# TensorE takes a slot's piece of the projections ahead of the residual's work and the down projection

## The reference

```python
h = layernorm(x) * (1 + ca) + sa
xn = norm(h) * norm_g + norm_b
# each direction (the second on the reversed sequence):
u, z = split(xn @ Win.T)                      # 256 and 256 channels
u = silu(conv4(u) + convb)
dtr, Bm, Cm = split(u @ Wx.T)                 # 8, 16, 16
dt = softplus(dtr @ Wdt.T + bdt)
h_t = exp(dt_t * A) * h_(t-1) + dt_t * u_t * B_t      # 16 states, 512 steps
y = (sum_n h_t * C_t + u * D) * silu(z);  y = y @ Wout.T
x = x + ga * (h + y_fwd + y_bwd)
h2 = layernorm(x) * (1 + cb) + sb
w = softmax over the two largest of h2 @ gate_w
out = shared(h2) + sum_e w_e * (silu(h2 @ w1_e) * (h2 @ w2_e)) @ w3_e     # hidden size 256
x = x + gb * out
```

## Time and profile before

| | us |
|---|---|
| median of three runs | 2583.36 (2583.35 to 2584.0) |
| the profiled execution, its own time | 2582.57 |
| its span, first to last instruction | 2580.8 |
| VectorE busy | 2284.9 (89%) |
| TensorE busy, matmuls | 2100.5 (81%) |
| GpSimd busy | 1957.8 (76%) |
| ScalarE busy | 1509.0 (58%) |

### The profile page before, as it was taken

The page is one execution under the profiler, slowest core; times in us unless marked ns, Lnnn a source line. Parts: engine busy times, 40 slices in busy tenths (PEclk is TensorE's granted clock), DMA queues, the critical chain, the costliest instruction groups (busy, mean ns, idle before and its releaser), DMA issues. The chain is left out here.

```text
span 2580.8 us, 31577 instructions
## 1 busy us (share of the span) xinstructions
PE 2100.5 (81%) x9893; PEld 1343.5 (52%) x9893; DVE 2284.9 (89%) x3603; ACT 1509.0 (58%) x2468; POOL 1957.8 (76%) x1437
## 2 busy tenths in 40 slices
PE   3677887978788897888879788897878879887868
PEld 1244554545555455555545555454555545555545
DVE  1699998999999899998989899899999989999973
ACT  2546656655566665656666555666556566555633
POOL 1577878778787877878877787877878787787854
PEclk8777998989899898998989899898989989899998
DMA  3334342333433333333333424333332433333310
GB/s 82 128 129 134 105 138 101 116 123 112 136 105 123 118 110 129 114 125 107 116 124 116 140 99 132 107 111 129 115 132 98 138 106 115 128 106 130 112 68 5
DMA packets 120557, 294.32 MB, mean 114 GB/s; under 512 B 18516, under 2 KB 53172, under 8 KB 120388
## 3 DMA queue, kind: packets, MB, share of 16 engines
q1 hardware_dynamic: 120388, 292.30, 33.7%
HBM read 285.91 MB, written 6.34 MB: 113 GB/s over the span
## 5 line engine op out<-in xcount | busy, mean ns | idle before, releaser
L426 POOL TENSOR_TENSOR bt<-v,bb 128x1024 f32<-128x1024 f32 x512 | 1208.4, 2363 | 158.7 <-DVE psA L787 154.6
L787 DVE TENSOR_TENSOR_SCAN psA<-psA,bt 128x512 f32<-128x512 f32 x1024 | 1197.3, 1215 | 100.7 <-POOL bt L426 81.1
L600 ACT ACTIVATE psA<-dt,aneg 128x512 f32<-128x512 f32 x1024 | 688.2, 688 | 813.0 <-DVE g L797 807.4
L987 PEld LDWEIGHTS psY<-ident,g 128*128 128x128 f32 x4096 | 515.4, 151 | 461.8 <-issue 241.6
L987 PE MATMUL psY<-ident,g 128*128 128x128 f32 x4096 | 605.5, 294 | 149.5 <-DVE g L797 149.4
L797 DVE TENSOR_TENSOR g<-psA,cb 128x512 f32<-128x512 f32 x1024 | 672.5, 676 | 0.0
L526 POOL TENSOR_TENSOR act<-pf,gf 128x512 f32<-128x512 f32 x288 | 366.8, 1273 | 248.4 <-DVE pf L882 216.2
L1068 PE MATMUL F<-h2T,w 128*128 128x512 f32 x576 | 333.9, 663 | 90.5 <-DVE pf L882 90.5
L1112 PE MATMUL F<-w,act 128*128 128x128 f32 x2304 | 319.8, 284 | 44.4 <-POOL act L526 41.1
L1112 PEld LDWEIGHTS F<-w,act 128*128 128x128 f32 x2304 | 292.2, 198 | 61.8 <-POOL act L526 55.3
L1071 PE MATMUL F<-h2T,w 128*128 128x512 f32 x576 | 307.5, 616 | 0.0
(11 more groups left out here) (133 smaller groups left out, 1709.1 us busy)
## 6 DMA issues: line engine op xcount, KB each, us to landing
bb<-bc_rows SPq DMA_DIRECT2D x256, 512.0 KB, 3.7
cb<-bc_rows SPq DMA_DIRECT2D x256, 512.0 KB, 3.6
x<-in_L_attn_x SPq DMA_DIRECT2D x16, 256.0 KB, 4.8
xR<-in_L_attn_x SPq DMA_DIRECT2D x16, 256.0 KB, 4.4
out_x<-osb SPq DMA_DIRECT2D x16, 256.0 KB, 4.8
w<-in_L_ffn_ew SPq DMA_DIRECT2D x2, 1024.0 KB
modA<-mod_table SPq DMA_DIRECT2D x16, 128.0 KB, 4.6
bc_rows<-xd SPq DMA_DIRECT2D x32, 64.0 KB, 3.2
```

What stands on the lines that cost most here:

```text
L426: g.tensor_tensor(bt[:, n % 2, :, :], v[d][:, :, :], bb[:, n // 2 % 2, n % 2, :].unsqueeze(1).broadcast_to([P, NH, T]), ALU.mult).then_inc ...
L600: s.activation(psA[:, half * T:half * T + T], dt_[d][:, half, :], ACT.Exp, scale=aneg[d][:, half, n:n + 1]).then_inc(a_s, 1)
L787: w.tensor_tensor_scan(ah, ah, bt[:, n % 2, half, :][:, order], 0.0, ALU.mult, ALU.add)\
L987: last = m.matmul(psY[:, half * T + i * P:half * T + i * P + P], g_[:, n % 2, half, i * P:i * P + P], ident[:, :], is_transpose=True, star ...
```

## The change

On TensorE alone, `ffn_late` moves behind `side` in each slot. `ffn_side` (the backward direction's turn of acc, slots 1 and 2), `sum_y` and `expert_up` stay where they are. No instruction is added or removed, and no wait is changed.

```diff
                     if ffn:
                         ffn_side(b - 1, slot)
-                        ffn_late(b - 1, slot)
                     if scan_:
                         side(b, slot, True, None if last else b + 1, True)
                     if ffn:
+                        ffn_late(b - 1, slot)
                         expert_up(b - 1, slot)
```

## The result

The changed kernel takes 2740.4 us (2739.9 to 2741.0) against 2583.4 us before: 1.061 times as long, 95% interval 1.059 to 1.062, or 157 us more where 112 were forecast. The direction was right, and the time lies 28 us above the range.

The account below looks back on a forecast made before the run. VectorE paces the scan, busy 142 us of a 152.67 us pass. 14 x 6.6 + 0.5 + 15 x 1.3 = 112.4 us on 2582.6 gave 2695, with 0.8 for the median 2696 us; range 2664 to 2712 us.

Parts of the forecast that it names:

- Slot 29: Down block of expert e=7 queues behind Z, which waits for zs; VectorE's sum starts 3.9 us later a pass.
- Slots 17, 20, 23, 25, 27 and 18, by their places: Down blocks end last in their pairs, so sums wait 1.0, 1.0, 0.5, 0.5, 0.2 us; slot 18 gains 0.5.
- Slots 8 to 10: Transposes into h2T wait for xb; ScalarE takes h2T 1.3 us later, arriving whole at the expert's tanh in slot 10.
- The step that failed: Slots 17 and 23: the pair ends where it did, so the sums wait 1.0 and 0.5 us.
- knock-on rival: Last expert's down block in slots 30 and 31 late by 1 us each pass: 2710 us; 6 in 100.
- GpSimd's waits absorb part: GpSimd runs on while VectorE stalls, shrinking VectorE's 4.9 us of waits for bt: 2627 us; 5 in 100.
- Order hardly matters: TensorE takes a ready block past a waiting one, so VectorE's sums wait for nothing: 2583 us; 2 in 100.
- faster: Tanh of z in slot 29 was waiting for TensorE, so earlier Z half 0 saves 1.61 us: 2553 us; 2 in 100.
- Full clock in slot 29: Z and the down block run at full clock, a term of 2.1 for 3.9 us: 2671 us; 6 in 100.
- h2T hidden: The 1.3 us delay of h2T in slots 8 to 10 costs nothing: 2676 us; 7 in 100.
- The wait for the expert sum: Sign: VectorE's wait ahead of the sum grows to about 100 us in the run, longest near 4 us in slot 29.

Follow-up runs that it names:

- the kernel with slot 29 alone: Kernel before, with the piece (`side`) moved ahead of the down projection (`ffn_late`) in slot 29 only; 2638.8 us.
- the fillers: Changed kernel plus idle-time matmuls on TensorE into F1, overwritten later, one in slot 16 and two in slot 21; 2697.5 us.
- The two passes of one execution above: Half-clock and full-clock passes of the kernel before with `side` ahead only in slots 3, 4, 16, 18, 22, 26, 28; 2581.6 us.

## Why the prediction was right and where it was wrong

**Slot 29**: forecast 3.9 us, measured 3.55. The mechanism holds step by step: Z behind zs, the down block behind Z, the wait for tanh unchanged, TensorE's idle time 5.06 us where 4.8 was forecast. The rest is the clock: TensorE got its full clock back within the down block, which took 1.59 us and not 1.85. Where the half clock lasts through it, as in most passes of the kernel with slot 29 alone, the wait is 3.88 us. The Trainium skill, "TensorE: Matmul & The Clock Gate", What overlaps and what doesn't (in Part 3), says that matmuls keep strict order. The trace agrees: the down block had its input at 1179.46 us and came behind Z, at 1186.36 us.

**Slots 17, 20, 23, 25, 27 and 18, by their places**: forecast 1.0, 1.0, 0.5, 0.5, 0.2 and -0.5 us; at full clock 0.97, 0.93, 0.39, 0.66, 0.25 and -0.52. Slot 23's rows gave 0.44, which the forecast rounded up. Slot 27's 0.25 bears out that it shares its delay with slot 25; slot 25's own 0.66 is 0.16 above its term, and no run says why.

**Slots 8 to 10**: forecast 1.3 us. ScalarE's h2T comes behind the transposes:

```profile
1072.89 1.11 PE L1093 MATMUL F<-ident,zF 128*128 128x128 f32 x4
...
1074.04 0.78 ACT L694 ACTIVATE h2T<-F,modC 128x512 f32<-128x512 f32 x1 [1.30 <-PE F L1093]
...
1077.18 2.35 DVE L787 TENSOR_TENSOR_SCAN psA<-psA,bt 128x512 f32<-128x512 f32 x2 [0.64 <-ACT psA L600]
...
1082.48 0.69 DVE L882 SCALAR_TENSOR_TENSOR pf<-tf,F 128x512 f32<-128x512 f32 x1 [2.38 <-ACT tf L681]
```

ScalarE's h2T waits 1.30 us, the delay that the forecast had. It was to arrive whole at pf, as a wait of 3.2 us. Instead 0.64 us of it meets VectorE at slot 10's scan and 0.44 at pf (2.38 against 1.94 us in the earlier trace rows), 1.1 in all.

**The step that failed** is the pricing of slots 17 and 23: "when both blocks are free to run, what follows the pair starts when it did", and the pair ends where it did. That took every block of TensorE at the clock it had in the trace of before. After the change the clock falls to 1.2 GHz in slots 16 and 21 of every full pass, and the down blocks behind it come 1.7 us later each: 3.4 us a pass, which is 163.84 against 160.4 us with the fillers, or 47 us over fourteen passes. (The two kernels' times differ by 43: the one with fillers is some 4 us longer ahead of pass 1 and behind pass 14.) With the fillers the kernel takes 2697 us, one above the forecast: the sum was right for a clock that the change did not leave as it was. The prediction weighed another clock in slot 29, as a gain, and in slots 30 and 31, and nowhere else. Its knock-on rival, slots 30 and 31, came to nothing: the last sum waits for nothing. It had also read that the lists of several passes show the same waits within about 0.1 us. The sum of slot 15 did not: 0.38 us in pass 6 and none in pass 7, because of the clock. That was the sign to be had beforehand. (The 981.61 us that it calls the start of pass 6 is the scan of slot 1; nothing rests on it.)

Smaller errors cancel in that 2697, so its closeness is in part luck: slot 29 was 0.4 us too high and slots 8 to 10 0.2, and 0.4 us of VectorE's own time were not in it. A pass is 7.8 us longer with the fillers, where 7.9 was forecast.

**The rivals.** That GpSimd's waits absorb part: no, VectorE's waits for bt did not shrink (81.1 and 82.4 us in the run). Order hardly matters, and faster: no. Full clock in slot 29 and h2T hidden: neither. The wait for the expert sum was to be 100 us in the run, and is 150.9.

What stays open is what fixes the place of a fall. The traces show that it isn't the gap just ahead of it alone (0.17 us in slot 14 of before, 1.17 and 2.05 us after, and no fall behind the same gaps in other passes or variants), and that within one execution passes with and without it run the same instructions and differ in where they lie in time. The Trainium skill, "TensorE: Matmul & The Clock Gate", Part 1, says that the chip's watch on TensorE's activity runs free of the kernel, so that the point at which the clock changes depends on where the first matmul happens to lie. The two passes of one execution above agree with that, but no run here moved the passes without changing anything else.

## What to carry to other kernels

Where one engine's queue holds both work whose reader waits now and work that waits for that reader, the waiting piece goes last. If it goes first, the reader waits for the waiting piece and then for its own block: in slot 29 Z's 2.08 and the down block's 1.59 us, less their overlap. TensorE's idle time of 5.06 us is not the price, since VectorE did not yet ask for the sum in it. The price is what VectorE, the engine that paces the kernel, waits once it asks. Try an order slot by slot and not for all slots at once; here one of fifteen slots gains and the loss is in seven (8, 17, 20, 23, 25, 27 and 29). And a sum made at the clock of the trace of before needs a second value at the other clock for every block that a reader will newly wait for, not only for those behind a long gap.

## What the runs showed of the hardware that I had not expected

TensorE's granted clock fell to 1.2 GHz behind gaps of 0.17, 1.2 and 2.1 us in otherwise busy work, and the same code behind the same gap ran at full clock in other passes. Extra matmuls in idle time made the changed kernel faster: by 44 us with one a pass in slot 16, 30 us with two in slot 21, 43 us with all three, and 60 us (2740 to 2680) with eight. A pass locked to one length, 163.8 us, from the third on, or went round in three lengths. And VectorE's busy time in a pass grew by 0.4 us with the same instructions; instructions behind a wait show longer by 10 to 20 ns each (a pair of scans 2.35 against 2.33 us), and they no longer overlap the one ahead (by 0.09 us between zs and the sum of slot 29 in the earlier trace rows). Five more such places a pass make 0.4 to 0.5 us, which is an estimate from these rows.
